# Graph kernel with two norms: the last pair handled graph by graph, adjacency and nodes asked for first in a step, another order of the first pairs

## What is computed

```python
Xw = X @ Wv + bv
e = leaky_relu(sj[:, None, :] + si[:, :, None] + ab[0], negative_slope=0.2)  # sj, si: Xw @ aw halves
alpha_matrix = A * exp(e)
transition = alpha_matrix / (sum(alpha_matrix, axis=-1, keepdims=True) + 1e-12)
H = 0; Xk = X
for k in range(3):
    H = H + Xk @ Wk[k] + bk[k]
    Xk = einsum('bij,bjd->bid', transition, Xk)
x = layernorm(x + relu(H))
x = layernorm(x + einsum('bnm,bmf->bnf', adj, x) @ w)
```

## Time and profile before

| what | us |
|---|---|
| median of three runs | 314.57 |
| the three runs | 315.82, 314.57, 312.14 |
| the profiled execution, whole | 313.07 |
| its span in the profile | 311.2 |
| PE busy (share of the span) | 283.3 (91%) |
| DVE, ACT, POOL busy | 222.8, 214.4, 216.7 |
| DMA queue of SP, share of 16 engines | 44.4% |

### The profile page before, as it was taken

The page is one execution under the profiler, slowest core; times in us unless marked ns, Lnnn a source line. Parts: engine busy times, 40 slices in busy tenths (PEclk is TensorE's granted clock), DMA queues, the critical chain, the costliest instruction groups (busy, mean ns, idle before and its releaser), DMA issues.

```text
span 311.2 us, 6748 instructions
## 1 busy us (share of the span) xinstructions
PE 283.3 (91%) x2259; PEld 277.0 (89%) x2259; DVE 222.8 (72%) x654; ACT 214.4 (69%) x515; POOL 216.7 (70%) x425
## 2 busy tenths in 40 slices
PE   4987899999999999999999999998999999887750
PEld 3977799999999999999999899998999999886650
DVE  4336578888888888888777667877787888767632
ACT  2376687788777777777888777768787777746300
POOL 2143738888888888878778787775887887657742
PEclk9999799999999999999999999999999999999955
DMA  6818554453564556553434445544554443350010
GB/s 176 297 36 152 119 117 156 130 156 69 125 150 154 144 148 154 152 152 112 92 126 141 148 153 154 152 135 127 113 119 116 98 120 112 121 180 8 35 67 34
DMA packets 28761, 39.28 MB, mean 126 GB/s; under 512 B 7219, under 2 KB 12342, under 8 KB 28726
## 3 DMA queue, kind: packets, MB, share of 16 engines
q1 hardware_dynamic: 27888, 38.32, 44.4%
q10 hardware_dynamic: 838, 0.53, 0.5%
HBM read 30.42 MB, written 8.42 MB: 125 GB/s over the span
## 4 chain that ended last, share of the span: by engine, by line
DMA 54%; SPq 13%; PE 13%; POOL 5%; ACT 5%; DVE 5%; issue 4%; POOLq 0%; ACTq 0%; DVEq 0%
DMA sj_rows_dram<-scores 51%; SPq L231 4%; SPq L236 4%; PE ps_v L648 3%; PE ps_y L648 3%; SPq L226 3%; SPq L248 2%; PE ps_out L648 2%; ACT y L361 2%; PE ps_h L648 2%; DMA spread<-sj_rows_dram 1%; DMA WvT_sb<-WvT_dram 1%; PE ps_agg L715 1%; DVE stats L520 1%; POOL rstd L585 1%
## 5 line engine op out<-in xcount | busy, mean ns | idle before, releaser
L622 POOL TENSOR_TENSOR y_lo<-y,y_hi 128x512 fp32r<-128x512 f32 x32 | 41.5, 1298 | 17.9 <-ACT y_hi L367 17.0
L609 POOL TENSOR_TENSOR XT_lo<-xt,XT_hi 128x512 fp32r<-128x512 f32 x32 | 41.3, 1291 | 15.7 <-ACT XT_hi L304 15.7
L371 ACT ACTIVATE agg_hi<-ps_agg 128x512 fp32r<-128x512 f32 x32 | 19.1, 598 | 36.6 <-PE ps_agg L717 36.6
L474 DVE TENSOR_TENSOR V_lo<-ps_v,V_hi 128x512 fp32r<-128x512 f32 x32 | 22.1, 690 | 27.0 <-ACT V_hi L354 26.9
L648 PE MATMUL ps_out<-w_hi,agg_hi 128*128 128x256 f32 x128 | 36.9, 288 | 4.4 <-DVE agg_lo L489 4.4
L648 PE MATMUL ps_y<-WY_hi,XT_hi 128*128 128x258 f32 x128 | 39.8, 311 | 1.2 <-DVE V_lo L479 1.2
L648 PE MATMUL ps_v<-WX_hi,XT_hi 128*128 128x256 f32 x128 | 38.7, 302 | 0.0
L361 ACT ACTIVATE y<-res,offset,rstd 128x256 f32<-128x256 f32 x64 | 34.7, 589 | 4.0 <-POOL offset L587 3.9
L648 PE MATMUL ps_v<-WX_hi,XT_lo 128*128 128x256 f32 x128 | 37.2, 290 | 0.0
L648 PE MATMUL ps_v<-WX_lo,XT_hi 128*128 128x256 f32 x128 | 37.0, 289 | 0.0
L648 PE MATMUL ps_y<-WY_hi,XT_lo 128*128 128x258 f32 x128 | 36.6, 286 | 0.0
(11 more groups left out here) (95 smaller groups left out, 1058.1 us busy)
## 6 DMA issues: line engine op xcount, KB each, us to landing
xt<-xt_dram SPq DMA_DIRECT2D x32, 256.0 KB, 6.3
adjs<-adjs_dram SPq DMA_DIRECT2D x32, 256.0 KB, 4.5
nodes<-nodes_dram SPq DMA_DIRECT2D x32, 256.0 KB, 4.4
out_dram<-out_sb SPq DMA_DIRECT2D x32, 256.0 KB, 7.0
spread<-sj_rows_dram SPq DMA_DIRECT2D x30, 128.0 KB, 4.1
Wk_sb<-Wk_dram SPq DMA_DIRECT2D x2, 256.0 KB, 5.5
sj_rows_dram<-scores SPq DMA_DIRECT2D x30, 1.0 KB, 6.7
WvT_sb<-WvT_dram ACTq DMA_DIRECT2D x1, 256.0 KB, 4.1
```

What stands on the lines that cost most here:

```text
L371: act.activation(agg_hi[:], ps_agg[:, :, :, 0], ACT.Copy).then_inc(agg_hi_ready, 1)
L474: dve.tensor_tensor(V1_lo[:], ps_v[:], V1_hi[:].bitcast(F32), ALU.subtract).then_inc(v1_lo_ready, 1)
L609: pool.tensor_tensor(XT_lo[k % 6][:].rearrange("p c b i -> p (c b i)"), xt_sb[k % 4][:], XT_hi[k % 6][:].rearrange("p c b i -> p (c b i)") ...
L622: pool.tensor_tensor(y_lo[:], y[k % 2][:], y_hi[:].bitcast(F32), ALU.subtract).then_inc(y_lo_ready, 1)
```

## The change

In the middle of the program only SyncE's order in a step changes: load_adjs(k+2), load_nodes(k+1), store(k-3), then load_spread(k+2), store_sj(k+3) and load_xt(k+8).

At the start: the low part of the first XT is made by VectorE and not by GpSimd, between the two parts of the split of Wk[2]; WvT is asked for ahead of the vectors; TensorE does only graph 0 of hop1(0) before it spreads the scores of pair 0, and graph 1 behind it; ScalarE makes TT_hi of pair 0 ahead of XT_hi of pair 3, and V1_hi of pair 0 ahead of the exponentials of pair 1; VectorE makes V1_lo of pair 0 ahead of the alphas of pair 1.

At the end: in the steps without hop2 (29 to 31) hop0 stands ahead of propagate_v2. Pair 31 (`LAST`) takes other banks (its h lies in ps_y, its two aggregates in ps_h and ps_v, its two outputs in ps_t and ps_agg) and buffers of its own, and from h on every piece is done for one graph at a time. Its normalisations and y_lo go from ScalarE and GpSimd to VectorE; normalise2 of pairs 29 and 30 goes from GpSimd to ScalarE; its output is stored in two halves, one from SP's queue and one from ACT's.

```diff
+        last_h = ps_y[:, :, 0:D]
+        last_agg = [ps_h[:].rearrange("p b (n i) -> p b n i", n=2), ps_v[:].rearrange("p b (n i) -> p b n i", n=2)]
+        last_out = [ps_t[:, 0:PER].rearrange("p b i -> p (b i)"), ps_agg[:, 0].rearrange("p b n i -> p (b n i)")[:, 0:D]]
...
             def load_xt(k):
-                if k >= 4:
-                    sp.wait_ge(xt_lo_ready, k - 3)
+                if k == 4:
+                    sp.wait_ge(xt0_lo_ready, 1)
+                if k > 4:
...
             def store(k):
-                sp.wait_ge(out_ready, k + 1)
+                if k < LAST - 2:
+                    sp.wait_ge(out_ready, k + 1)
+                else:
+                    sp.wait_ge(late_out_ready, k - (LAST - 2) + 1)
...
             def step(k):
+                if there(k + 2) and k >= 0:
+                    load_adjs(k + 2)
+                if there(k + 1) and k >= 0:
+                    load_nodes(k + 1)
+                if there(k - 3):
+                    store(k - 3)
                 if there(k + 2) and k + 2 >= BY_PE:
                     load_spread(k + 2)
-                if there(k + 1) and k >= 0:
-                    load_nodes(k + 1)
-                if there(k + 2) and k >= 0:
-                    load_adjs(k + 2)
-                if there(k - 3):
-                    store(k - 3)
                 if there(k + 3) and k + 3 >= BY_PE:
                     store_sj(k + 3)
                 if there(k + 8) and k >= -4:
                     load_xt(k + 8)
...
+            for k in range(-5, LAST + 3):
+                step(k)
+            sp.wait_ge(last_out_ready, 1)
+            sp.dma_start(out[LAST, :, 0:D], out_sb[LAST % 2][:, 0]).then_inc(last_stored, DMA)
...
+            act.dma_start(WvT_sb[:], WvT.rearrange("(c p) n -> p c n", p=P)).then_inc(WvT_loaded, DMA)
             act.dma_start(vectors_sb[:].rearrange("p c n -> p (c n)"), vectors).then_inc(vectors_loaded, DMA)
-            act.dma_start(WvT_sb[:], WvT.rearrange("(c p) n -> p c n", p=P)).then_inc(WvT_loaded, DMA)
             act.dma_start(ab_col[:], ab.partition_broadcast(P)).then_inc(ab_loaded, DMA)
...
+            def late_normalise2(k):
+                act.wait_ge(offset2_ready, k + 1)
+                act.wait_ge(stored[k % 2], loads(k - 2))
+                for b in range(PER):
+                    last = act.activation(out_sb[k % 2][:, b], res2[:, b], ACT.Identity, bias=offset2[:, b:b + 1],
+                                          scale=rstd2[:, b:b + 1])
+                last.then_inc(late_out_ready, 1)
...
                     tt_hi(k)
                 if there(k + 1):
                     leaky_of(k + 1)
+                    if k == 0:
...
                 if there(k + 3):
                     scores_of(k + 3)
-                if there(k):
...
@@ -412,13 +474,22 @@
             transition(0)
             scores_of(1)
             v2_hi(1)
+            tt_hi(0)
             xt_hi(3)
-            tt_hi(0)
             scores_of(2)
             v2_hi(2)
             xt_hi(4)
-            for k in range(PAIRS + 3):
+            for k in range(PAIRS):
                 step(k)
+            aggregate_hi(LAST - 1)
+            late_normalise2(LAST - 2)
+            for b in range(PER):
+                last_y_hi(b)
+            for b in range(PER):
+                last_aggregate_hi(b)
+            late_normalise2(LAST - 1)
+            act.wait_ge(last_out_ready, PER)
+            act.dma_start(out[LAST, :, D:2 * D], out_sb[LAST % 2][:, 1]).then_inc(last_stored, DMA)
 
...
+                              XT_hi[0][:].rearrange("p c b i -> p (c b i)").bitcast(F32),
+                              ALU.subtract).then_inc(xt0_lo_ready, 1)
+            dve.wait_ge(WY_hi_ready, 1)
+            dve.tensor_tensor(WY_lo[:, :, 0:D], Wk_sb[:, 2], WY_hi[:, :, 0:D].bitcast(F32), ALU.subtract)
 
             dve.wait_ge(u_done, 1)
             split(WY_hi[:, :, D:D + 2], WY_lo[:, :, D:D + 2], ps_u).then_inc(WY_ready, 1)
...
                     tt_lo(k)
                 if there(k - 2):
                     aggregate_lo(k - 2)
-                if there(k + 1):
+                if there(k + 1) and k > 0:
                     alphas(k + 1)
-                if there(k):
-                    v1_lo(k)
+                v1_lo(k)
+                if there(k + 1) and k == 0:
...
@@ -562,8 +700,35 @@
             v2_lo(1)
             tt_lo(0)
             v2_lo(2)
-            for k in range(PAIRS + 3):
+            for k in range(PAIRS):
                 step(k)
+            last_residual1(0)
+            last_statistics1(0)
+            last_residual1(1)
+            last_moments1(0)
+            aggregate_rest(LAST - 1)
+            last_statistics1(1)
+            aggregate_lo(LAST - 1)
+            last_moments1(1)
+            for b in range(PER):
+                last_normalise1(b)
+            for b in range(PER):
+                last_y_lo(b)
+            for b in range(PER):
+                last_aggregate_rest(b)
+                last_aggregate_lo(b)
+            residual2(LAST - 1)
+            for b in range(PER):
+                statistics2(LAST - 1, b)
+            moments2_of(LAST - 1)
+            last_residual2(0)
+            last_statistics2(0)
+            last_mom2(0)
+            last_residual2(1)
+            last_statistics2(1)
+            last_mom2(1)
+            for b in range(PER):
+                last_normalise2(b)
 
...
                 if there(k - 1):
                     at_lo(k - 1)
                     norm1(k - 1)
                 if there(k - 3):
                     normalise2(k - 3)
-                if there(k + 4) and k >= 0:
...
-            for k in range(4):
+            for k in range(1, 4):
                 xt_lo(k)
-            for k in range(PAIRS + 3):
+            for k in range(PAIRS):
                 step(k)
+            for b in range(PER):
+                last_norm1(b)
+            at_lo(LAST)
+            norm2(LAST - 1)
+            for b in range(PER):
+                last_norm2(b)
 
...
+            def last_aggregate(b):
+                if b == 0:
+                    pe.wait_ge(at_lo_ready, PAIRS)
+                pe.wait_ge(last_y_lo_ready, b + 1)
+                for c in range(C):
+                    cols = slice(c * P, (c + 1) * P)
+                    pe.matmul(last_agg[b][:, c].rearrange("p n i -> p (n i)"), y_hi[:, b, cols], AT_parts[LAST % 2][:, b],
+                              start=True, stop=False, skip_group_check=True)
+                    last = pe.matmul(last_agg[b][:, c, 1], y_lo[:, b, cols], AT_parts[LAST % 2][:, b, 0],
+                                     start=False, stop=True, skip_group_check=True)
+                last.then_inc(last_agg_done, 1)
...
+            def last_project(b):
+                pe.wait_ge(last_agg_lo_ready, b + 1)
+                for c in range(C):
+                    last = product(last_out[b], (last_agg_hi[:, b, c], last_agg_lo[:, b, c]),
+                                   (w_hi[:, c], w_lo[:, c]), c == 0, c == C - 1)
+                last.then_inc(last_out_done, 1)
...
             def step(k):
-                if there(k):
-                    if k > 0:
-                        hop1(k)
-                        transpose_t(k)
-                if there(k + 3) and k > 0:
+                if k > 0:
+                    hop1(k)
+                    transpose_t(k)
+                if k > 0 and there(k + 3):
                     hop2_and_scores(k + 3)
-                if there(k):
-                    propagate_v2(k)
+                if not there(k + 3):
+                    hop0(k)
+                propagate_v2(k)
                 if there(k - 2):
                     if k == 2:
                         pe.wait_ge(w_ready, 1)
                     project(k - 2)
                 if k == 0:
                     hop2_and_scores(3)
-                if there(k):
-                    if k > 0:
-                        hop0(k)
-                    propagate_v1(k)
+                if k > 0 and there(k + 3):
+                    hop0(k)
+                propagate_v1(k)
                 if there(k - 1):
                     aggregate(k - 1)
...
@@ -776,17 +987,23 @@
             pe.wait_ge(WY_ready, 1)
             hop2_and_scores(0)
             pe.wait_ge(WX_ready, 1)
-            hop1(0)
+            hop1(0, [0])
             pe.wait_ge(identity_ready, 1)
             spread_scores(0)
+            hop1(0, [1])
             hop2_and_scores(1)
             pe.wait_ge(WX_ready, 2)
             hop0(0)
             spread_scores(1)
             transpose_t(0)
             hop2_and_scores(2)
-            for k in range(PAIRS + 3):
+            for k in range(PAIRS):
                 step(k)
+            project(LAST - 1)
+            for b in range(PER):
+                last_aggregate(b)
+            for b in range(PER):
+                last_project(b)
 
```

151 lines of the change are left out of this document (130 added, 21 removed).

## The result

The changed kernel takes 300.52 us (median; 298.93 to 300.88), the kernel before on the same chip 313.36 (312.09 to 315.82): a ratio of 0.957 with a 95% interval of 0.949 to 0.965. The prediction was 300.5. The profiled execution took 300.44 with a span of 298.6, against 311.2 before. In a later set of runs, on a chip on which the kernel before took 326.64, the changed kernel took 300.72, a ratio of 0.923: it is the kernel before that differs between the sets, with 313 to 327 us, while the changed one stays at 300.5 and 300.7. Some executions are over 1.5% longer than the fastest of the same kernel (two of the four of y_v1_late, the profiled one of x_sp); the medians in this document include them, the ratios leave them out.

The account below looks back on a forecast made before the run. Bound by TensorE up to 160 us, SP's round for the next 66, and dependent chains at both ends. -4.4 - 1.8 - 2.5 - 4.5 = -13.2 from 313.07 gives 299.9, set at 300.5 us; 296.5 to 306 holds 8 in 10.

Parts of the forecast that it names:

- The middle, -4.4: Pairs 15 to 29: SP's round becomes about 7.1 us, below TensorE's 8.28 us step, recovering all 4.4 us lost.
- the 5 I took: Middle: the spread's assumed landing time in us with a store just ahead, between bounds 4.1 and 7.0; its cover is 6.3.
- Leaky's wait for the spread in the middle: Middle: the prediction is wrong if ScalarE's leaky waits for the spread there; no size given.
- rival 2: Middle: the store ahead makes the spread land too late, 0.7 us in some 28 steps, about 319 us; chance 0.05.
- rival 3: Middle: the scores' landing grows to 8.7 us, so the kernel stays within 1%, 314 to 317 us; chance 0.08.
- The start, -1.8: First pairs: propagate_v1(1), at 33.60 us, comes 1.8 us earlier; bounds -0.2 and -3.4.
- The low stretch near 35 us: Start: a 3.9 us stretch at clock 0.58 loses 1.6 us; one more gives -0.2, one less -3.4.
- the 1.7 us at the spread of pair 0's scores: Start: with 6 instead of 12 hop1(0) matmuls in front, TensorE reaches this spread by 12.8 instead of 14.45 us.
- the gain at 33.60 is that of the spread, 1.4: Start: pair 2's scores, spread and leaky come 1.4 us earlier, so propagate_v1(1) does; 0.3 to 0.4 more follows.
- asking for WvT first: Start: requesting WvT first gives up to 0.4 us, within 1.0 to 1.4 gained at hop2(2).
- Pairs 29 to 31, -2.5: Last steps: hop0 fills TensorE's wait, norm engines set the pace; two steps take 15.5 instead of 18.07; bounds -1.5, -3.1.
- The tail, -4.5: From pair 31's transposes to the end: 21.9 us instead of 26.4, by pieces per graph; bounds -2.5 and -6.

Follow-up runs that it names:

- y_v1_late: Kernel after with V1_hi of pair 0 and the alphas of pair 1 back in their old places: 301.31 us, ratio 0.918 of before.
- x_sp: Kernel before with only SyncE's new order (adjacency, nodes and store ahead of the spread): 306.39 us, ratio 0.973.
- x_sj: Kernel before with the scores' store right behind the spread, then nodes, adjacency and store: 306.25 us, ratio 0.974.
- y_sp_undone: Kernel after with SyncE's old order in a step: 313.15 us, ratio 0.995 of before.
- x_start: Kernel before with only the new order of the first pairs, SyncE's order old: 316.36 us, ratio 1.002.
- after_again: Kernel after, unchanged, run again in a later set on another chip: 300.72 us, ratio 0.923 of before.
- y_extra2: Kernel after with two more 256 KB loads, which nobody reads, ahead of each spread: 310.18 us, ratio 0.980 of before.
- x_sp_start: Kernel before with SyncE's new order and the new order of the first pairs, old end: 305.60 us, ratio 0.974.
- x_sp_start_hop0: Kernel before with SyncE's new order, the new start, and hop0 ahead of propagate_v2 in steps 29 to 31: 306.08 us, ratio 0.967.
- y_sj: Kernel after with TensorE spreading a third pair's scores and SyncE issuing spread and scores' store first: 298.24 us, ratio 0.949 of before.
- y_both: Kernel after with TensorE spreading a third pair's scores and pair 30's second norm earlier on VectorE: 299.16 us, ratio 0.918 of before.

## Why the prediction was right

**The middle, -4.4: right (-4.06), and for its reason.** x_sj has the short round without the early adjacency and gets 115.92; y_sp_undone, which has everything but SP's order, takes 123.45, and x_start with the start alone 124.81. The spread was issued at 3.2 us as worked out, and landed after 4.1, less than the 5 I took. Of the missing 0.35 (116.27 against 115.92), 0.24 is one step of 8.52, in which leaky waited 0.51 us for the spread; in after_again one step took 9.89, with a largest landing of 7.4. Leaky's wait for the spread in the middle is one of the signs by which I would have called the prediction wrong: it shows, small, in single steps. That is rival 2 in one step of 28, a risk to each execution that the price of "each of some 28 steps" had no place for; y_extra2 shows that a late spread is paid once and doesn't come back.

**The scores' landing.** I said that the sum doesn't need it to shrink. It shrank from 6.7 to 4.6 us, so rival 3, which had it grow, was on the wrong side. The gain doesn't hang on it: in y_extra2 the scores land after 6.4 and SP keeps up. What stands ahead in the queue goes with the landing in all runs. In the old order spread, nodes, adjacency and store were issued within 1.8 us, the store lands after 6.9 to 7.1 and the scores behind it after 6.7 to 6.9; x_sj issues nodes, adjacency and store together as well, and its store takes 5.6. In the new order SP waits 2 us between nodes and store (112.53 to 114.57), the store lands after 2.4 to 3.0, and the scores after 4.5 to 4.9; with two more loads ahead (y_extra2) they take 6.4.

**The start, -1.8: the size came out by luck (-1.56 at propagate_v1(1), -1.24 at pair 15), the working didn't.** The rows for it, propagate_v1(1) in x_start and in after_again, then TensorE's clock from 35.0 to 38.9 us in the kernel after and in after_again:

```profile
32.22 0.38 PE L662 MATMUL ps_h<-V_hi,TT_hi 128*128 128x256 f32 x1 [1.19 <-DVE V_lo L486]
...
33.34 0.39 PE L835 MATMUL ps_h<-V_hi,TT_hi 128*128 128x256 f32 x1 [2.52 <-DVE V_lo L551]
```

```profile
35.00:38.90 3.90, 3.90 (x28) 3.90 (x28) 1.55 (x3) 2.33 (x6) 2.37 (x5) 0.76 0.42 158
...
35.00:38.90 3.90, 3.90 (x35) 3.90 (x35) 2.83 (x9) 2.57 (x7) 2.76 (x6) 1.00 0.60 132
```

- *The clock's rise.* TensorE rose to full pace at 15.09 us in the profiled execution before and at 12.90 in that after. At half pace these 2.2 us are worth up to 1.1, most of the 1.54 by which T(0) is earlier. It isn't the change's doing, since the kernel after showed 12.90 once and 15.47 the other time, and the old start 11.76, 14.64 and 15.09.
- *The new order* gives 0.4 to 0.9 us at T(0) (after_again beside before, 18.43 against 18.61 though its rise is 0.4 later; y_v1_late beside x_sp, 17.75 against 18.69 at nearly the same rise), and 0.9 from there to propagate_v1(1): 14.05 us after T(0) in x_start, 14.99 in the kernel before. Together that is 1.3 to 1.9, about the 1.8 I took. But the way there was mis-sized. The spread of pair 0's scores can't be 1.7 earlier: the six matmuls in front take 1.0 to 1.3 by the prediction's own numbers, and it is reached only that much earlier (13.06 instead of 14.45, with an earlier rise).
- *SP's order at the start* I put at nothing, without a reason. Adjacency and nodes now stand ahead of the first spread, the nodes' issue held the queue for 2.37 us, the spread left 3.7 us after the scores' store and landed 5.0 us later (leaky(2) starts at 28.49): 8.8 together, where x_start took 7.5. TensorE then waits longer ahead of propagate_v1(1), which starts 14.91 to 15.29 us after T(0) in the five profiled executions with both edits (after, after_again, x_sp_start, x_sp_start_hop0, y_v1_late), where it is 14.02 in y_sp_undone and 14.05 in x_start. So 0.9 to 1.3 us are given back, nearly all that the order had gained behind T(0).
- *The low stretch near 35 us.* From propagate_v1(1) to T(3) the kernels without extra loads take either 11.5 to 11.9 us, at a granted clock of 1.00, or 13.1 to 13.5, with a stretch below: 1.5 us. The pair of profiles has one such stretch on either side (0.58 before, 0.76 after, from 35.0 to 38.9 us), neither one more nor one less, so it cancels, as the sum had assumed. It isn't the longer wait that brings it: TensorE waited 2.09 us in the kernel after and fell, 2.52 in after_again and didn't, and 1.18 in the kernel before and fell. Most of the 2.45 us by which x_start is faster than before from T(0) to T(3) is this stretch and not the order. What decides about it stays open.

The steps of the prediction that failed are the 1.7 us at the spread of pair 0's scores, "the gain at 33.60 is that of the spread, 1.4", which left out what SP's new order takes back, and that of asking for WvT first, "up to 0.4": u's matmul started at 5.30 instead of 5.38, since it now waits for the other of its two operands, the vectors.

**Pairs 29 to 31, -2.5: right (-2.48), the split other than the prediction's words have it.** 1.84 is SP's lateness (x_sj, x_sp_start and x_start all take 16.23; x_start has the old order, but its SP had caught up by then), 0.5 to 0.6 is hop0, to which the prediction gave most of it. The steps are 7.87 and 7.72, inside or just above the 7.5 to 7.8 of the norm engines, and the chain that ended last runs through these engines there; that they set the pace was not tried by itself.

**The tail, -4.5: right.** In the pair of profiles -4.82; over all kernels the old tail takes 25.5 to 26.6 and the new one 21.2 to 22.0, 4.5 apart in their middles. The clock has a part in the spread: before had 0.50 in its tail and after 0.81 from 282.7 to 288.1 us and 0.86 to 293.0, while y_v1_late, with 0.70 and then 0.50 from 11 us behind the transposes on, takes 21.97, which is 4.4 less than before. By pieces: residual1 at 5.73 after the transposes (predicted 5.75), aggregate at 11.09 (11.0), project at 13.48 (13.2), end at 21.59 (21.9).

**The sum.** -1.24 - 4.06 - 2.48 - 4.82 = -12.6 against -13.2; 300.44 measured against 299.9 for the profiled execution. That the median then came at 300.52 beside a forecast of 300.5 is luck as far as it is nearer than this: the start's terms erred both ways, and the clock's rise helped by up to 1.1.

## What to carry to other kernels

Add up the round of a queue that waits for its own transfers, and compare it with the step: while it is longer, gains elsewhere are lost again (x_start), and its lag shows as a wait for whatever comes last in the queue, not for what caused it. When issues are moved ahead of a waiting one, give the request with the longest round trip the most cover: y_sj, whose spread has 4.2 us more, has no long step in the middle, where y_both, which asks for the largest loads first, has one of 9.29. Compare the parts of two profiles at the same granted clock, or a rise or a fall that one execution has and the other hasn't will be credited to the change.
